# Splitting the reciprocals of the step sizes into quarters of 128 columns and spreading them over the program

## What is computed

```
mod = (silu(c) @ wmod) -> sa, ca, ga, sb, cb, gb      # ga, gb are held away from 0
h = layernorm(x) * (1 + ca) + sa
x = x + ga * attn(h)                                   # a Mamba2 layer
h = layernorm(x) * (1 + cb) + sb
x = x + gb * (h @ binarized(weight) + bias)

attn: xBC, z, A_log = split(h @ in_proj)               # 64 heads of 16 channels, 8 groups, state 64
      x, B, C = silu(conv1d(xBC, 4 taps) + bias)
      dt   = softplus(A_log)                           # the step sizes, one per token and head
      x_in = x / dt
      y    = chunked_scan(x_in * dt, -dt, B, C) + D * x_in
      out  = (y * silu(z + z_bias)) @ out_proj
```

## Time and profile before

| | |
|---|---|
| time, median of 3 runs | 655.74 us (654.91 to 656.59) |
| profiled execution | 658.04 us, its span 656.3 us |
| PE matmul busy | 612.0 us, 93% of the span |
| VectorE busy | 504.1 us, 77% |
| ScalarE busy | 383.8 us, 58% |
| GpSimd busy | 355.8 us, 54% |
| mean granted TensorE clock | 0.990 of 2.4 GHz |

### The profile page before, as it was taken

The page is one execution under the profiler, slowest core; times in us unless marked ns, Lnnn a source line. Parts: engine busy times, 40 slices in busy tenths (PEclk is TensorE's granted clock), DMA queues, the critical chain, the costliest instruction groups (busy, mean ns, idle before and its releaser), DMA issues.

```text
span 656.3 us, 21241 instructions
## 1 busy us (share of the span) xinstructions
PE 612.0 (93%) x8345; PEld 481.2 (73%) x8345; DVE 504.1 (77%) x928; ACT 383.8 (58%) x844; POOL 355.8 (54%) x411
## 2 busy tenths in 40 slices
PE   2788899999999999999999999999997999999995
PEld 1565677787787777878777787787875777888884
DVE  6797799978778787787977778778695566787756
ACT  2788555456465455655545655656664437566565
POOL 4776114347537355554543755547574657766642
PEclk9799999999999999999999999999999999999999
DMA  8734120613221221421222253231325735444411
GB/s 296 224 131 163 39 67 29 203 66 103 67 92 60 83 72 54 148 74 41 70 76 100 88 152 102 70 120 64 97 71 166 224 106 147 137 129 128 129 49 64
DMA packets 59866, 70.52 MB, mean 107 GB/s; under 512 B 13972, under 2 KB 33460, under 8 KB 59256
## 3 DMA queue, kind: packets, MB, share of 16 engines
q1 hardware_dynamic: 59768, 69.17, 33.0%
HBM read 54.45 MB, written 14.70 MB: 105 GB/s over the span
## 4 chain that ended last, share of the span: by engine, by line
PE 78%; DVE 7%; POOL 4%; issue 4%; ACT 3%; DMA 3%; SPq 1%; POOLq 0%; DVEq 0%; ACTq 0%
PE bank L1218 37%; PE bank L1985 12%; PE pair L1283 7%; PE bank L1227 4%; PE bank L2018 4%; PE pair L1256 3%; PE bank L1313 2%; PE bank L1236 2%; PE pair L1269 2%; DVE m_cv L1472 1%; POOL h_lo L435 1%; PE pair L1296 1%; DMA h_lo_place<-y_scratch 1%; PE bank L1245 1%; DVE p_xn L514 1%
## 5 line engine op out<-in xcount | busy, mean ns | idle before, releaser
L1472 DVE SCALAR_TENSOR_TENSOR m_cv<-bank,gpc,m_cv 128x511 f32<-128x511 f32 (+2 forms) x192 | 143.5, 748 | 36.0 <-ACT m_cv L1375 31.5
L1218 PE MATMUL bank<-h_hi,w_hi 128*128 128x512 f32 x384 | 163.2, 425 | 1.6 <-POOL h_lo L435 1.5
L1218 PE MATMUL bank<-h_hi,w_lo 128*128 128x512 f32 x384 | 152.0, 396 | 0.0
L1218 PE MATMUL bank<-h_lo,w_hi 128*128 128x512 f32 x384 | 151.4, 394 | 0.0
L1387 ACT ACTIVATE m_M<-bank 128x512 f32<-128x512 f32 x128 | 76.1, 594 | 65.9 <-PE bank L1227 64.1
L1375 ACT ACTIVATE m_cv<-bank,gpc 128x512 f32<-128x512 f32 x96 | 72.0, 750 | 72.6 <-PE bank L1218 72.1
L1614 POOL TENSOR_TENSOR m_S<-m_S,m_cd 128x128 f32<-128x128 f32 x96 | 40.2, 419 | 126.5 <-DVE m_S L1535 65.4
L1218 PEld LDWEIGHTS bank<-h_hi,w_hi 128*128 128x128 f32 x384 | 73.1, 190 | 22.1 <-issue 3.1
L1604 POOL TENSOR_TENSOR m_Xw<-m_Xp,wend 128x256 f32<-128x256 f32 x64 | 39.8, 622 | 85.4 <-ACT m_Xp L1395 85.4
L1218 PEld LDWEIGHTS bank<-h_hi,w_lo 128*128 128x128 f32 x384 | 72.5, 189 | 16.7
L1502 DVE TENSOR_TENSOR m_M<-m_M,pair 128x512 f32<-128x512 f32 x128 | 81.8, 680 | 0.3 <-issue 0.3
(11 more groups left out here) (179 smaller groups left out, 1228.9 us busy)
## 6 DMA issues: line engine op xcount, KB each, us to landing
m_ea<-ea_scratch SPq DMA_DIRECT2D x32, 256.0 KB
m_dd<-dd_scratch SPq DMA_DIRECT2D x32, 256.0 KB
y_scratch<-m_t SPq DMA_DIRECT2D x16, 512.0 KB, 3.4
h_lo_place<-y_scratch SPq DMA_DIRECT2D x16, 512.0 KB, 4.5
p_wm<-in_L_wmod_dram SPq DMA_DIRECT2D x6, 1024.0 KB, 6.7
m_wraw<-in_L_attn_in_proj_w_dram SPq DMA_DIRECT2D x18, 256.0 KB, 3.4
w_lo_place<-in_L_attn_input__dram SPq DMA_DIRECT2D x16, 256.0 KB, 4.8
out_dram<-t_o SPq DMA_DIRECT2D x16, 256.0 KB, 2.3
```

The lines of the kernel that those rows point to most:

```text
L1218: ins = pe.matmul(A[k % 3][:, :], w[:, t, kc, :], h[:, n % NB, kc, :], start=(m == 0), stop=(m == 11))
L1472: ins = dve.scalar_tensor_tensor(out=cv[:, k % 3, lag:], in0=A[k % 3][:, 0:L - lag], scalar=s.gpc[:, gp, o:o + 1], in1=cv[:, k % 3, lag:], ...
```

## The change

The reciprocal and its multiplication are cut into four pieces of 128 columns, each a pair of instructions; each piece first waits until the step sizes are there. For pair 0, pieces 0 and 1 now stand at the end of `start.vector`, and pieces 2 and 3 where the whole stood, at (-1, 1). For pair 1, the pieces stand at slot 3 of units 3, 4, 5 and 6, in place of the whole at (4, 3). SP's store of pair 1 moves from v == 5 to v == 6, and its semaphore counts 8 per pair in place of 2.

```
     def store_skips(sp, pb):
-        sp.wait_ge(a_skip, 2 * pb + 2)
+        sp.wait_ge(a_skip, 8 * pb + 8)
...
         silu(2)
         silu(3)
+        skips(dve, 0, range(0, 2))
...
-    def skips(dve, pb):
-
-        dt = s.chain[:, pb, 0, :]
-        dve.reciprocal(dt, dt).then_inc(a_skip, 1)
-        dve.wait_ge(a_skip, 2 * pb + 1)
-        dve.tensor_scalar(dt, dt, dcol[:, 0:1], None, ALU.mult).then_inc(a_skip, 1)
+    def skips(dve, pb, these):
+
+        for k in these:
+            dt = s.chain[:, pb, 0, k * P:(k + 1) * P]
+            chained(dve, pb, A_DT)
+            dve.reciprocal(dt, dt).then_inc(a_skip, 1)
+            dve.wait_ge(a_skip, 8 * pb + 2 * k + 1)
+            dve.tensor_scalar(dt, dt, dcol[:, 0:1], None, ALU.mult).then_inc(a_skip, 1)
...
-                if v == 5:
+                if v == 6:
                     start.store_skips(sp, 1)
...
                     if (v, sl) == (-1, 1):
-                        start.skips(dve, 0)
+                        start.skips(dve, 0, range(2, 4))
...
-                    if (v, sl) == (4, 3):
-                        start.skips(dve, 1)
+                    if 3 <= v < 7 and sl == 3:
+                        start.skips(dve, 1, range(v - 3, v - 2))
```

## The result

The changed kernel is slower. Its time is 660.89 us in the median of 9 runs (658.17 to 664.34) against 655.74 us of 9 before (653.26 to 660.70), so the medians lie 5.2 us apart; the ratio is 1.0071, 95% interval 1.0048 to 1.0094, so 3.2 to 6.2 us, middle 4.7. In a second comparison (experiment nine) it was 1.0072 (1.0045 to 1.0100). The prediction said 657.6 us, range 655.2 to 659.2, with 0.37 for slower by over 0.3%.

A forecast was written before the change was run, and what follows sets the result against it. The prediction took PE at full clock as the bound from 200 us on, and before that a chain through VectorE. Terms +2.3 + 1.1 - 1.5 = +1.9 us on 655.74 gave 657.6 us, range 655.2 to 659.2.

The forecast's parts named there:

- The quarters ahead of `mod_t`: At pair 0's start, two quarters of 1.14 us delay `mod_t`, and ScalarE and PE behind it: +2.3 us.
- What is freed at unit -1: Two of pair 0's quarters leave (-1, 1), inside VectorE's 4.3 us wait for PE: gives nothing.
- The clock: PE's longer idle stretch before the second decay matmul brings a further fall to 1.2 GHz behind it: +1.1 us.
- rows 6: Profile rows before the change: granted clock at 0.50 from about 79.7 to 82.9 us, taking 1.7 us.
- The second place: Pair 1's quarters at units 3 to 6 remove PE's 1.64 us wait before unit 6's diagonal: -1.5 us.
- The 0.3 us feared at unit 8: PE waits 0.3 us before unit 8's diagonal because of the quarter at (6, 3), unless `m_dd` lands sooner.
- SP's queue: Pair 1's store, landing in 4.2 to 6.0 us, delays loads behind it, hidden by 2 to 5 us: 0.
- The sum: All terms over the whole kernel: +2.3 + 1.1 - 1.5 = +1.9 us.
- the rival 'faster': Longer waits shift the fall at 79.7 to 82.9 onto idle time, regaining 1.7 us: -0.9 us, 654.8; chance 0.12.

The follow-up runs named there:

- experiment nine: The changed kernel measured again, nothing altered, beside the kernel before: 661.44 us, ratio 1.0072.
- fifth experiment: Kernel before with only pair 0 in quarters, plus 15 unread matmuls in PE's idle stretch before the second decay matmul: 658.73 us, ratio 1.0040.
- second experiment: Kernel before with only pair 0 in quarters, two ahead of `mod_t`; pair 1 and its store as before: 661.74 us, ratio 1.0088.
- fourth: Changed kernel plus 15 unread matmuls in PE's idle stretch before the second decay matmul: 658.54 us, ratio 1.0038.
- third experiment: Changed kernel with pair 0's first two quarters moved behind the gate values, so behind `mod_t`: 656.79 us, ratio 1.0001.
- one: Changed kernel with pair 0 left whole at unit -1, so only pair 1 in quarters: 655.14 us, ratio 0.9982.
- eight, 6 matmuls: Changed kernel plus 6 unread matmuls at the head of PE's idle stretch before the second decay matmul: 658.66 us, ratio 1.0031.
- six, one quarter: Kernel before with only pair 0 in quarters, one ahead of `mod_t` and three at unit -1: 658.14 us, ratio 1.0021.
- seven, four quarters: Kernel before with only pair 0 in quarters, all four ahead of `mod_t`: 663.47 us, ratio 1.0100.

## Why the prediction was wrong

**The quarters ahead of `mod_t`: right.** Forecast 2.3 us, measured 2.36 in the trace; the fifth experiment, in which the clock stays up, costs 2.6 us. A quarter takes 1.18 us, not 1.14: the reciprocal 0.94 (0.95 forecast), the multiplication 0.29 (0.24). What is freed at unit -1 gives nothing, as forecast; it is 1.4 us (one piece took 3.8, two quarters take 2.4) and not the 2.2 that the prediction gave VectorE's wait there, a slip that its sum doesn't use.

**The clock: the right mechanism, the wrong size, and this is the step that failed.** "From below nothing, from above the 1.7 us of rows 6. I take 1.1 us, since a part of the fall will lie over idle time". The trace has 2.78 us of work lost on the chain, and the second and fifth experiments, 1.0088 and 1.0040, differ by 3.2. The low stretch behind 3.32 us of idle time lasted 6.8 us, about twice that of the earlier trace rows (3.4 us, from 79.5 and not from 79.7 as the prediction read it; its 1.7 us are right), and 6.1 us of it lay over work. The upper bound was wrong in kind: it took one fall, behind a stretch of 1.88 us, as the most that any fall could cost. In the earlier trace rows PE had been at work again for 1.5 us when the clock fell; here it fell while PE still stood idle, and all four profiles in which that happened show 6.8 us. The mean granted clocks of the runs agree, without a trace. Of the span, (1 - clock) times its length is 5.8 us in the kernel before (0.9912 in the mean of its 21 runs of the last comparison) and 8.8 us in the changed one (0.9867, 6 runs): 3.0 us more. In the second experiment it is 8.7 us against 5.7, in the fifth 4.9 us (0.9925). These means carry about 1 us of scatter, since the profiles have further low stretches before 44 us and around 500 us that come and go.

**The second place: right in kind, a little small.** Forecast -1.5 us. In the profile -1.13 at unit 6 and -1.2 by unit 8; by the ratios, 1.0088 less 1.0071 is 1.1 us, and pair 1 alone gave 0.9982, 1.2 us; the margins are over 2 us and 1.2 us. The 0.3 us feared at unit 8 didn't come, for the reason that the prediction allowed for (`m_dd` landing sooner); a wait of 0.36 us came at 124.71 instead, which the text had not looked for: it followed `m_M` through the four slots, and not `m_xs`, for which a projection waits. The fourth and fifth experiments, 1.0038 and 1.0040, show next to nothing of this gain; their intervals are 0.002 wide to either side and hold it still.

**SP's queue: right.** Nothing behind the moved store waits for it. The landing took 2.0 us, less than the 4.2 taken as least.

**The sum.** +2.4 + 3.0 (between the 2.78 of the trace and the 3.2 of the experiments) - 1.2 = +4.2 us against 4.7 measured, inside its interval of 3.2 to 6.2.

**A second weakness: one execution stood for the kernel.** The profiled execution before had a second fall, 79.5 to 82.9, behind 1.88 us of idle time. The forecast drew its upper bound from it, and the rival 'faster' its 1.7 us to win back; as shown above, that fall was worth 0.9. The same stretch of 1.88 us stands in eleven profiles of this study (in the other two it was filled), and the clock fell behind it in three of them (before the change, second and third experiment) and not in eight. The Trainium skill ("TensorE: Matmul & The Clock Gate", Part 1) says that the point at which steady work brings the full clock varies from run to run; the prediction quoted this and said that no row showed it. The eleven profiles show such a variation for the fall, which doesn't even come each time.

What stays open: what decides in one execution whether and when the clock falls behind a stretch of about 2 us, and whether the last 0.5 us of the sum are more than noise.

## What to carry to other kernels

A wait that lands on TensorE while it works for the critical chain costs its own length and can cost the clock behind it, here in some profiles from about 2 us of idle time on and in each of the four with over 3 us; 2.4 us of VectorE work put ahead of a small instruction cost 5.8 us. Before a piece is moved out of one place, look at what it waits beside: pair 0's reciprocal was hidden in a wait of 4.3 us, and its two quarters were put at the one place around it where VectorE had no slack; behind the next few instructions they cost nothing that could be told (third experiment). For an effect that comes and goes between executions, one trace bounds nothing: compare several, or the mean clocks of all runs.

## What the runs showed of the hardware

The length of PE's idle stretch at the first place, and the clock behind it, one profile each:

| kernel | idle stretch, us | clock low, us | of it over PE's work | that work takes, us |
|---|---|---|---|---|
| before, one and three | 0.96 to 0.97 | none | | 4.91 to 4.92 |
| eight, 6 matmuls | 2.29 | none | | 4.92 |
| six, one quarter | 2.14 | 74.9 to 78.3, 3.4 | all | 6.48 |
| after | 3.32 | 73.6 to 80.4, 6.8 | 6.1 | 7.69 |
| two, pair 0 alone | 3.33 | 73.8 to 80.6, 6.8 | 6.4 | 7.81 |
| nine, after again | 3.33 | 74.6 to 81.4, 6.8 | 5.6 | 7.45 |
| seven, four quarters | 5.70 | 72.0 to 78.8, 6.8 | 3.1 | 6.35 |
| four and five, 15 matmuls | 0.71, 0.72 | none | | 4.91 |

The work is that from the second decay matmul to the next idle stretch. Each microsecond of it at 1.2 GHz costs 0.45 to 0.47 us (7.69 - 4.91 = 2.78 us for 6.1, 1.57 for 3.4).

A stretch of 2.29 us without a fall stands beside one of 2.14 with it, so in this range the length alone doesn't decide. What goes with the length of the low stretch is what PE was doing when it began. In the four profiles where the clock fell while PE still stood idle it stayed low for 6.8 us; in the four falls where PE was back at work, in one of them for 0.1 us only (six, and the three behind the stretch of 1.88 us), for 3.4 us. Why is open.

A reciprocal costs (3.34 - 0.94) / 384 columns = 6.3 ns per column and about 0.14 us per instruction.
